# Three moves in the hand-written step orders of a macaron transformer kernel on one core

## What is computed

```python
def ffn(x, ...):                       # two layers, DEPTH = 2
    for l in range(2):
        h = shift_token(x)             # upper half of the features from the token before
        q, k, v = split(h @ wqkv[l])   # 8 heads of 64
        q, k = rotary_xpos(l2norm(q) * qs[l], l2norm(k) * ks[l])
        o = local_attention(q, k, v)   # blocks of 128 tokens, each sees itself and the one before
        x = x + o @ wo[l]
        a, g = split((layernorm(shift_token(x)) * lg[l] + lb[l]) @ w1[l] + b1[l])
        x = x + (a * gelu(g)) @ w2[l] + b2[l]
    return x

x = x + 0.5 * ffn(layernorm(x))
x = x + attn(layernorm(x), weight)     # 16 heads of 16, 512 x 512 scores, weight (4096, 256)
x = x + 0.5 * ffn(layernorm(x))
```

## Time and profile before

| | |
|---|---|
| median of 3 runs | 3581.15 us |
| the profiled execution's own time | 3581.15 us |
| its span in the trace | 3579.4 us |
| PE busy | 3407.0 us (95%) |
| VectorE (DVE) busy | 2588.1 us (72%) |
| ScalarE (ACT) busy | 2077.3 us (58%) |
| GpSimd (POOL) busy | 2265.4 us (63%) |
| chain that ended last | PE 78%, DVE 6%, issue 4%, DMA 4% |

### The profile page before, as it was taken

One profiled execution on the slowest core, in us unless ns is written; L12 is line 12 of the kernel. 1 busy time (PEld: TensorE's weight loads), 2 busy tenths in 40 slices (PEclk: granted clock), 3 DMA queues, 4 the chain that ended last, 5 costly groups with the idle time before them and its releaser, 6 DMA issues.

```text
span 3579.4 us, 69415 instructions
## 1 busy us (share of the span) xinstructions
PE 3407.0 (95%) x20896; PEld 2792.8 (78%) x20896; DVE 2588.1 (72%) x7106; ACT 2077.3 (58%) x4860; POOL 2265.4 (63%) x2319
## 2 busy tenths in 40 slices
PE   4899999999998799999999999998999999999997
PEld 3678778778777588888888888886777877777875
DVE  5887888988887365565555656656888788888884
ACT  1676776776775344444444444434677677677673
POOL 3577678677675355555555555574767777767762
PEclk9899999999999899999999999998999999999998
DMA  5444344455355331222212122212434445445433
GB/s 167 134 151 147 126 153 150 148 162 160 125 161 165 78 69 48 48 49 48 60 48 42 49 53 57 75 30 89 160 126 152 144 135 170 159 125 163 157 122 112
DMA packets 429686, 404.44 MB, mean 113 GB/s; under 512 B 139896, under 2 KB 374360, under 8 KB 429304
## 3 DMA queue, kind: packets, MB, share of 16 engines
q1 hardware_dynamic: 429304, 399.89, 37.0%
HBM read 226.07 MB, written 159.38 MB: 108 GB/s over the span
## 4 chain that ended last, share of the span: by engine, by line
PE 78%; DVE 6%; issue 4%; DMA 4%; POOL 3%; SPq 3%; ACT 2%; DVEq 0%; POOLq 0%; ACTq 0%
PE psum L1543 21%; PE psum L1544 20%; PE psum L1545 20%; PE psum L1680 5%; PE psum L1663 5%; PE psum L1772 3%; PE psum L1652 2%; POOL ge_lo L889 1%; DMA pT<-p_turned 1%; DVE probs L1246 1%; SPq L614 1%; ACT probs L992 1%; DMA w_hi<-w_lo 1%; PE psum L1700 1%; PE psum L1726 1%
## 5 line engine op out<-in xcount | busy, mean ns | idle before, releaser
L889 POOL TENSOR_TENSOR ge_lo<-ge,ge_hi 128x512 fp32r<-128x512 f32 x512 | 673.3, 1318 | 526.9 <-PE psum L1545 285.3
L1069 ACT ACTIVATE ge<-psum 128x512 f32<-128x512 f32 x512 | 307.0, 600 | 669.5 <-PE psum L1772 669.4
L850 POOL TENSOR_SCALAR probs<-probs,rz 128x256 f32<-128x256 f32 (+1 forms) x1024 | 446.6, 457 | 376.7 <-DVE rz L1260 375.8
L1439 DVE CAST ge_hi<-ge 128x512 fp32r<-128x512 f32 x512 | 264.9, 520 | 507.6 <-ACT ge L1069 505.2
L992 ACT ACTIVATE probs<-probs,nb,rq 128x256 f32<-128x256 f32 (+1 forms) x1024 | 577.4, 573 | 21.5 <-DVE nb L1254 19.7
L825 POOL TENSOR_TENSOR rinv<-ssq,minus_half 128x16 f32<-128x16 f32 x124 | 361.8, 2927 | 27.9 <-DVE ssq L1230 27.6
L1246 DVE CUSTOM_DVE_ANT_0 probs<-psum,mask 128x256 f32<-128x256 f32 (+1 forms) x1024 | 339.0, 387 | 55.5 <-PE psum L1663 40.7
L1543 PE MATMUL psum<-wqkv_hi,hT_hi 128*128 128x512 f32 x768 | 326.8, 426 | 13.9 <-DVE hT_lo L1202 7.3
L1268 DVE STREAM_TRANSPOSE p_blocks<-probs 128x384 f32<-128x384 f32 (+1 forms) x384 | 292.2, 786 | 47.5 <-POOL probs L850 26.1
L1544 PE MATMUL psum<-wqkv_hi,hT_lo 128*128 128x512 f32 x768 | 307.6, 401 | 0.0
L1545 PE MATMUL psum<-wqkv_lo,hT_hi 128*128 128x512 f32 x768 | 306.8, 399 | 0.0
(11 more groups left out here) (163 smaller groups left out, 9693.0 us busy)
## 6 DMA issues: line engine op xcount, KB each, us to landing
p_turned<-p_blocks SPq DMA_DIRECT2D x128, 512.0 KB, 2.9
pT<-p_turned SPq DMA_DIRECT2D x512, 128.0 KB, 2.9
p_turned<-p_blocks SPq DMA_DIRECT2D x128, 384.0 KB, 3.1
pT<-p_turned SPq DMA_DIRECT2D x512, 96.0 KB, 2.4
xnext<-stream SPq DMA_DIRECT2D x32, 512.0 KB, 3.9
xmid<-stream SPq DMA_DIRECT2D x32, 512.0 KB, 3.9
gaT<-y_turned SPq DMA_DIRECT2D x256, 64.0 KB, 2.0
y_turned<-probs SPq DMA_DIRECT2D x192, 64.0 KB, 2.9
```

The costliest lines, as they stand in the source:

```text
L850: last = nc.gpsimd.tensor_scalar(pu, pu, rz[:, h, t:t + 1], 1.0, ALU.mult, ALU.mult)
L889: nc.gpsimd.tensor_tensor(ges[1][:, k % 4, :], ge[:, k % 4, :], f32(ges[0][:, k % 4, :]), ALU.subtract).then_inc(S["g_lo"], 1)
L1069: nc.scalar.activation(ge[:, k % 4, :], RB[k % 2], ACT.Exp, scale=GSCALE, accum_out=gz[:, h, t:t + 1]).then_inc(S["g_exp"], 1)
```

## The change

Three lists and the code of one step are edited.

1. `wf2` moves in `SP_STEPS` from behind `ld7` to between `ld4` and `ld5`.
2. `P2` moves in `DVE_STEPS` from in front of `ik f1` to behind them.
3. `-F0`, which stood in front of P0, and `-F1`, which stood in front of `-e`, become one step `-F` in front of `-e` that does both halves and raises `dve_old` once. The two waits on `dve_old` count by one instead of two.

```diff
 DVE_STEPS = ("X0 -j0 -j1 +zl0 +zl1 X1 R0 -nl0 -nl1 X2 R1 V0 X3 V1 -y0 R2 -y1 +rq0 +rk0 -y2 V2 X4 R3 X5 R4 V3 "
-             "-y3 X6 +ss0 V4 R5 X7 V5 -F0 P0 B +rq1 R6 +rk1 +ss1 -y4 R7 V6 -y5 V7 i2 +ss2 P1 f0 iv -F1 -e +rk2 "
-             "+rq2 P2 ik f1 P3 +ss3 iq x +rk3 +Y l +rq3 r f2").split()
+             "-y3 X6 +ss0 V4 R5 X7 V5 P0 B +rq1 R6 +rk1 +ss1 -y4 R7 V6 -y5 V7 i2 +ss2 P1 f0 iv -F -e +rk2 +rq2 "
+             "ik f1 P2 P3 +ss3 iq x +rk3 +Y l +rq3 r f2").split()

-SP_STEPS = ("+xin wq wo wf0 wf1 st0 st1 ld0 -hs ld1 wr -old st2 st3 ld2 ld3 st4 st5 ld4 ld5 st6 st7 ld6 ld7 "
-            "wf2 -keep res shift").split()
+SP_STEPS = ("+xin wq wo wf0 wf1 st0 st1 ld0 -hs ld1 wr -old st2 st3 ld2 ld3 st4 st5 ld4 wf2 ld5 st6 st7 ld6 "
+            "ld7 -keep res shift").split()
...
-            need(sp, S["dve_old"], 2 * m)
+            need(sp, S["dve_old"], m)
...
                         dve.wait_ge(S["xold_in"], 16 * (m + 1 - final))
-                        xv = xmid[:, 2 * i:2 * i + 2, :].rearrange("p t d -> p (t d)")
-                        last = V.scalar_tensor_tensor(xv, xv, 0.5, nrm[:, 2 * i:2 * i + 2, :].rearrange("p t d -> p (t d)"),
+                        for b in range(2):
+                            xv = xmid[:, 2 * b:2 * b + 2, :].rearrange("p t d -> p (t d)")
+                            last = V.scalar_tensor_tensor(xv, xv, 0.5, nrm[:, 2 * b:2 * b + 2, :].rearrange("p t d -> p (t d)"),
                                                           ALU.mult, ALU.add)
                         last.then_inc(S["dve_old"], 1)
...
-                    dve.wait_ge(S["dve_old"], 2 * m + 2)
+                    dve.wait_ge(S["dve_old"], m + 1)
```

## The result

Four runs of the kernel after have a median of 3625.06 us (3621.71 to 3628.97), four of the kernel before 3580.02 us (3576.89 to 3583.39): ratio 1.0126 (95% interval 1.0108 to 1.0144), 45 us slower. The forecast was 25 us slower, with a range that ended at 3613. The sign was right, the size too small.

The account below looks back on a forecast made before the run. The prediction took PE, holding 78% of the chain, as the bound. Terms 14.5 (rounds 8, 24) + 3.9 (0) + 2.0 (16) + 4.4 (6, 22) + 0 (F) = 24.8 us on 3581.15 gave 3606 us, range 3594 to 3613.

Parts of the forecast that it names:

- The hold and its place: Rounds 8 and 24: SP stands at wf2 for i2, A5 starts 6.2 us late, 5.05 us left after W0's wait goes.
- the late end's 1.7: Rounds 8 and 24: delay of ld5 if all of w2's transfer stands in front, at most 1.7 us; 0.5 taken.
- The clock: Rounds 8 and 24: PE's idle time before A5 lowers its granted clock, 1.5 us per round, bounds 0 and twice that.
- q3 behind P2 in these rounds: Rounds 8 and 24: f1 now precedes P2, which ends at 694.8 against q3 at 694.1, 0.7 us more each.
- Edit 3 at 0: Final rounds: joint F in front of e makes e 0 to 0.2 us later, W0 still covered, cost 0.
- The forecast's own doubt: Final rounds: the prediction would be wrong if they differ by over 0.3 us each.
- Rounds 6 and 22: P2 behind ik makes q3 wait 2.2 us in each round, 4.4 us in all.
- Round 0: f1 ahead of P2 makes q3 late, 2.4 us left, plus 1.5 us for the clock: 3.9 us.
- Round 16: f1 ahead of P2 makes q3 2.0 us late, an idle time too short to lower the clock.
- the transfer in rounds 0 and 16 at 0: wf2's issue and transfer ahead of ld5 are covered by PE's waits: 0, or 1 us if that cover is short.

Follow-up runs that it names:

- experiment 5: Kernel before, with SP waiting between ld4 and ld5 for the cast that frees w2's buffer, w2's DMAs staying behind ld7: 3591.69 us against 3583.43.
- experiment 3: Kernel before with only F changed, both halves in one step in front of e: 3592.85 us, 12.0 more, ratio 1.0035.
- experiment 2: Kernel before with only P2 moved behind ik and f1: 3589.70 us, 8.9 more, ratio 1.0028.
- experiment 11: Kernel after, but with both halves of F in front of P0: 3609.16 us against 3580.84 for the kernel before, ratio 1.0077.
- experiment 12: Kernel before with P2 moved behind ik in rounds 6 and 22 alone: 3589.68 us, 8.8 more, ratio 1.0023.
- experiment 6: Kernel before with w2's loads between ld4 and ld5 only in rounds 0 and 16: 3585.01 us against 3583.43, ratio 1.0007.
- experiment 1: Kernel before with only wf2 moved between ld4 and ld5: 3601.23 us against 3580.85, ratio 1.0058.
- experiment 7: Kernel before with joint F in front of e, only multiplying, without adding the old x: 3584.17 us against 3583.43, ratio 1.0004.
- experiment 8: Kernel before with the joint F placed behind V7, some 5 us before e: 3584.00 us against 3583.43, ratio 1.0008.

## Why the prediction was too small

Its steps, with what the table and the runs say:

- **The hold and its place: right.** wf2 stands for `i2`, PE waits for pT in front of A5, W0's 1.15 us go. Terms per round 8 and 24: A5 late 6.2 forecast, a wait of 6.89 measured, because ld5 landed 4.1 us after its issue. I took 0.5 us for w2 in front and had 1.7 as bound; 1.0 to 1.2 was it (experiment 5 has 3.1 us from the last ld5 issue to A5 without w2, 2.9). The Trainium skill (DMA: Bandwidth & Descriptors, section on queues, rings and completion order) says that descriptors on one engine's ring are consumed in ring order, but also that a later one may finish its write before an earlier one; so "cannot overtake", as the forecast has it, is more than the page gives. The delay lies between my 0.5 and the late end's 1.7, and no run tells waiting in order from a shared bandwidth.
- **The clock: its size was wrong.** I counted the A5 block once, 1.5 us. Measured: A5's 12 matmuls 1.98 us against 1.09 at full clock (0.9), and the w block behind them from 688.49 to 692.66 = 4.17 us against 681.22 - 678.31 = 2.91 (1.3): 2.2 us a round.
- **q3 behind P2 in these rounds: 1.52 forecast as 0.7.** The step from e to f1 is 697.16 - 692.87 = 4.3 us and not 3.7, as `e` now runs so late that K0 is what the next step waits for, and `e` starts 1.54 us before W0 and not 1.85. Together for a round: 6.89 + 2.2 - 1.15 - 0.3 (PE's wait for hid_lo, now covered) + 1.52 = 9.2, against 7.25 forecast; 4 us short for both.
- **Edit 3 at 0: the step that failed most.** The forecast said that F in front of e takes "0.65 us or, beside GpSimd, up to 1.0 us more", so that `e` is "0 to 0.2 us later" and W0's cover holds. The pair took 2.70 us, 1.4 more than alone. I had bounded it by the longest single F before (1008 ns), of which there was never more than one in front of `e`; of two in a row one takes about 1.0 us and the other up to 1.78. `e` then starts 1.17 us behind k3's start (831.33) and not 0.20 (818.39 - 818.19), so it is about 1.0 us late. The cover was overrated too: I set 1.85 us of k3 and K0 against 1.29 of `e`, but it is 1.75 against 0.20 of late start, 1.29 and 0.05 until W0, a slack of 0.21. The rest, 0.77 us, is what W0 is late. It is found at W0 in the 12 final rounds that have a next element's K0 in front of it, 9.7 us in all; experiment 3 alone measured 12.0. The forecast's own doubt ("final rounds that differ by over 0.3 us each") was the case that came.
- **Rounds 6 and 22: the wait was right, the clock wrong.** 2.2 us forecast, 2.19 measured. I had let one row of 2.20 us idle with a full clock behind it stand as the rule. In four traces with P2 behind `ik` (after, experiments 2, 11, 12), eight such waits of 2.18 or 2.19 us, the stretch grew by 3.5 to 3.8 us in six and by 1.9 to 2.0 in two, round 22 of experiments 2 and 11, where the granted clock stayed 1.00 behind the wait. 7.1 us here against 4.4.
- **Round 0: 3.9 forecast, nothing measured.** f1 took 2.77 us there, not 4.85, and A5 and A7 waited for pT (2.90 and 0.76 us) behind w2, so that P2 was in time but for 0.48 us. How far that hides a loss can't be read from two traces: in the nine traces with no edit in round 0 this same stretch took 208.3 to 212.5 us, before's being the longest, and in those with P2 moved there (experiment 2, after, experiment 11) 210.9, 211.8 and 213.8. One cause is the clock ahead of the edits: in the window from 130 to 135 us the granted clock was 0.50 in before and 1.00 in after. So 3.9 us is not seen, and that nothing was measured is partly luck.
- **Round 16: 2.0 forecast, 4.7 in the stretch.** The q3 wait that I forecast was 0.33 us, since A7 in front of it waits 1.95 us for pT: a late load took its place. I had put the transfer in rounds 0 and 16 at 0 because PE's waits behind A5 cover it. They cover A5's part; A7's has no cover (experiment 6). From PE's first A step of the round on, after is 6.3 us longer than before (99.7 against 93.3); the attention part in front of it was 1.6 us shorter, which is within what it moves by in traces without an edit there.

Summed over the stretches: 24.8 + 4.1 (rounds 8, 24) + 2.7 (6, 22) + 2.7 (16) + 13.1 (final rounds) - 4.6 (round 0) + 0.2 (the others) = 43.0, the difference of the spans; the times give 45. Of the 13.1 us, 9.7 are W0's wait for `e`; traces without any edit of F have 3.4 (experiment 1) and 2.7 us (experiment 2) more than before in the same stretches, so the other 3.4 need no cause in F. F is the largest part of what was missing.

Does edit 1 split into its parts? By the times not quite: alone it is 20.4 us, its hold alone 8.3 and its transfer in rounds 0 and 16 alone 1.6, which leaves 10.5. By the stretches it does: 7.5 + 7.0 + 3.6 = 18.1 us, against 5.6 + 4.8 = 10.4 for the hold, 3.9 for the transfer in round 16, and 4.1 left for the transfer in rounds 8 and 24 (no run has that one by itself). Times and stretches differ by 2 us or so in each of the three kernels, which is within their intervals (3 to 5 us each way).

## What to carry to other kernels

A wait put into a hand-written queue is paid by everything behind it: before moving a load forward, look for the event that frees its buffer, and for who needs the entries it now stands ahead of. Price an instruction in a new place by what the neighbour engine does at that moment, not by its longest duration elsewhere; two in a row can both meet the neighbour's work. When a step is to be "covered", count the cover from the start of the one step to the start of the other in the rows, late starts included. And where a new wait of PE may lower the granted clock, as 2.19 us did in six of eight cases here, price it twice, as the wait and as the slower matmuls behind it, with both ends in the range.

## What the runs showed of the hardware

- VectorE's F and GpSimd's products held each other up: F's pair 1.28 us beside short products, 2.70 beside full ones, and GpSimd's L820 1.74 us beside an F (in before beside F1 as well), 1.30 with none beside it (experiment 8). The Trainium skill (SBUF — State Buffer, section "Who interferes with whom") says that a VectorE instruction with two SBUF inputs contends with a GpSimd instruction that reads SBUF, as an exclusive lock, and that a tensor_scalar which enters a two-port mode does so too; by that rule, the trace agrees, for the pair of experiment 7 as well: 0.405 us at the shortest and 2.17 us for two beside GpSimd. That its tensor_scalar was in such a mode is inferred.
- After the same idle time of 2.18 or 2.19 us PE's granted clock fell to the half in six of eight cases; after the 4.51 us of experiment 5 and the 6.89 us of after (round 8) it was 0.51 and 0.50 in the window behind.
- 128 KB loads issued right behind w2's 682 KB reached PE 4.1 us after their last issue, against 3.1 us without it (experiment 5).
